# Softmax denominators of the last four slots: summed by TensorE per chunk instead of by GpSimd

## Chip, cores and metric

The kernel runs on one core of a Trainium2 chip. The metric is the device time of one execution in microseconds (us). Before the change it is 1859.81 us, the median of three runs (1859.74 to 1862.59). The chip's engines go by these names below: PE is TensorE (PEld its weight loads), DVE is VectorE, ACT is ScalarE, POOL is GpSimd, SP issues the DMAs.

## What is computed

One layer of a perceiver: a cross attention, a differential self attention and a mixture of eight experts, each added to the running `x`. Only the cross attention is touched. Cut to it, the reference is:

```python
q = (query @ wq.T + bq).reshape(B, SQ, H, HD).transpose(0, 2, 1, 3)
k = (key @ wk.T + bk).reshape(B, -1, H, HD).transpose(0, 2, 1, 3)
v = (value @ wv.T + bv).reshape(B, -1, H, HD).transpose(0, 2, 1, 3)
scores = jnp.einsum('bhqd,bhkd->bhqk', q, k) / jnp.sqrt(HD)
attn = jax.nn.softmax(scores, axis=-1)
ctx = jnp.einsum('bhqk,bhkd->bhqd', attn, v)
```

Here B = 8 batches, 128 queries, 2048 keys, 16 heads of 32 (HD), width 512, all in float32.

## The kernel before

`cross_attention` cuts the attention into 32 **slots**, one for each batch and group of four heads, and each slot into four **chunks** of 512 keys, so chunk number n = 4·slot + c runs from 0 to 127. All engines follow one hand-written calendar of **beats**: functions such as `score_step(beat)` or `value_step(beat)` say which chunk has its turn at a beat, and each engine walks over the beats in program order, waiting on semaphores where it needs another engine. A slot takes eight beats. For 32 · 8 beats TensorE also projects the keys and values (`keys`, `values`, `transposes`), one unit at each beat, and this fills it. From beat 256 on the projections are over, and slots 28 to 31 are still to be finished; that stretch is called the **tail** here.

What happens to a chunk, with the lines of the profile:

- PE, `column_scores` (L587): 16 matmuls write scores, keys on the partitions, to the PSUM tile `psS`. There is one such tile, so PE waits until ACT has moved the chunk before (`s_moved`).
- DVE (L759, L762): four maxima over `psS` into `mx`.
- ACT, "move" (L713): copies `psS` to one of six buffers of `s` (`BUFS = 6`), so it waits for the readers of chunk n − 6.
- Once in a slot, PE turns `mx` (`turn("M", ...)`, L619), DVE reduces it (L726), ACT spreads it (L700), PE turns it back (`turn("B", ...)`), ACT copies it to `mb` (L692).
- DVE (L733): subtracts `mb` from the chunk. ACT (L705): the exponential, in place.
- PE, `outputs` (L601): 16 matmuls add values times exponentials to `psO[:, 0:P]`.
- POOL (L512, L517): sums the exponentials of the slot's 16 key tiles into `acc`; 7 additions of 128x1024 in a slot, two for each chunk but the first, which has one.
- PE, `denominators` (L611): when POOL has finished the slot, 8 matmuls with a block of ones sum `acc` over the partitions into `psO[:, P:2*P]`.
- DVE (L740, L742, L747): reciprocal, product and bias of the slot; SP writes it to `o_scratch`.

The order of DVE at an even beat is: reduction, subtraction of chunk n, the slot's end, maxima of chunk n + 5. The order of PE is: `outputs`, `denominators`, `column_scores`, projection, turns. The units that pass through PSUM (transposes, projections, the two turns) use three banks `work` in turn, by a table RING made in advance:

```python
        BANKS = 3
        RING = {}
        for beat in range(FIRST, LAST):
            if (x0 := transposed(beat)) is not None:
                RING["T", *x0] = len(RING)
```

After the cross attention comes a barrier, and then `output_projection` (its transposes are L772, its products L43 to L45, POOL's additions L831).

Of the kernel before, what the change touches and what calls it, by code (L numbers as in the profile page):

```python
# [11 lines left out]
ACT = mybir.ActivationFunctionType  # L12
# [3 lines left out]
P = 128  # L16
B = 8
# [300 lines left out]
def cross_attention(nc, x, ctx_in, w, q_d, o_d, cin, shared):  # L318

    with ExitStack() as ctx:  # L320
# [12 lines left out]
        ADDS = 2 * CHUNK - 1  # L333
        MAXIMA = CHUNK * CHUNK

        def steps(beat, first, every, count):

            n, r = divmod(beat - first, every)
            return n if r == 0 and 0 <= n < count else None
# [32 lines left out]
        def sum_slot(beat):  # L372
            return steps(beat, 40, SLOT, SLOTS)
# [3 lines left out]


        BANKS = 3
        RING = {}  # L380
        for beat in range(FIRST, LAST):
            if (x0 := transposed(beat)) is not None:
                RING["T", *x0] = len(RING)
            if (x0 := projected(beat)) is not None:
                p0, u0 = x0
                RING["KV"[u0 // CHUNK], p0, u0 % CHUNK] = len(RING)
            if (s0 := turned_slot(beat)) is not None:
                RING["M", s0, 0] = len(RING)
            if (s0 := spread_slot(beat)) is not None:
                RING["B", s0, 0] = len(RING)  # L390
        UNITS = list(RING)

        def key_place(b, g, c):

# [106 lines left out]
        @block.gpsimd  # L501
        def _(pool):
            nc.gpsimd.memset(ones[:, :], 1.0).then_inc(const, 1)
            for n in range(SLOTS * CHUNK):
                m, c = divmod(n, CHUNK)
                buf = n % BUFS
                pool.wait_ge(exp_done, n + 1)
                if c == 0:

                    if m:  # L510
                        pool.wait_ge(od_full, m)
                    nc.gpsimd.tensor_tensor(acc[:, :, :], s[:, buf, 0:2, :], s[:, buf, 2:4, :],  # L512
                                            ALU.add).then_inc(sum_done, 1)
# [12 lines left out]
        def _(pe):  # L526
            pe.wait_ge(const, 1)

            def bank_of(unit):
                i = RING[unit]  # L530
                if i >= BANKS:
                    kind, m, n = UNITS[i - BANKS]
                    if kind == "T":
                        pe.wait_ge(split_done, m * CHUNK + n + 1)
                    elif kind == "K":
                        pe.wait_ge(k_done, m * CHUNK + n + 1)
                    elif kind == "V":
                        pe.wait_ge(v_done, m * CHUNK + n + 1)
                    elif kind == "M":
                        pe.wait_ge(top_done, m + 1)  # L540
                    else:
                        pe.wait_ge(mb_done, m + 1)
                return work[i % BANKS]

            def transposes(p, n):
                h, kk = divmod(n, 2)
# [44 lines left out]
            def outputs(n):  # L591
                m, c = divmod(n, CHUNK)
                b, g = divmod(m, G)
                pe.wait_ge(v_done, (b * CHUNK + c + 1) * CHUNK)
                if c == 0 and m:
                    pe.wait_ge(od_free, m)
                pe.wait_ge(exp_done, n + 1)
                for i in range(CHUNK):
                    at = value_places(b, c * CHUNK + i)[g]
                    for j in range(HG):  # L600
                        last = nc.tensor.matmul(psO[j * HD:(j + 1) * HD, 0:P],  # L601
                                                v[:, at + j * HD:at + (j + 1) * HD],
                                                s[:, n % BUFS, i, j * P:(j + 1) * P],
                                                start=c == 0 and i == 0, stop=c == CHUNK - 1 and i == CHUNK - 1)
                last.then_inc(pv_done, 1)

            def denominators(m):
                pe.wait_ge(sum_done, (m + 1) * ADDS)
# [13 lines left out]
            for beat in range(FIRST, LAST):  # L622
                if (x0 := transposed(beat)) is not None:
                    transposes(*x0)
                if (n := value_step(beat)) is not None:
                    outputs(n)
                if (m := sum_slot(beat)) is not None:
                    denominators(m)
                if (n := score_step(beat)) is not None:
                    column_scores(n)  # L630
                if (x0 := projected(beat)) is not None:
                    p, u = x0
                    if u < CHUNK:
# [17 lines left out]
        def _(act):  # L651
            act.wait_ge(bias_in, 32)
            for beat in range(FIRST, LAST):
                if (x0 := projected(beat - 1)) is not None:
                    p, u = x0
                    b, c = divmod(p, CHUNK)
                    if u < CHUNK:
                        i = RING["K", p, u]
                        act.wait_ge(work_full, i + 1)
                        if b:  # L660

                            act.wait_ge(s_full, ((b - 1) * G + c) * CHUNK + u + 1)
                        at = key_place(b, u, c)
                        nc.scalar.activation(kT[:, at:at + 512], work[i % BANKS][:, :], ACT.Identity,  # L664
                                             bias=bk[:, u:u + 1]).then_inc(k_done, 1)
                    else:
                        u -= CHUNK
                        i = RING["V", p, u]
                        act.wait_ge(work_full, i + 1)
                        if b:  # L670

# [1 line left out]
                        at = value_places(b, c * CHUNK + u)  # L673
                        step = at[1] - at[0]
                        if step == P:
                            nc.scalar.activation(v[:, at[0]:at[0] + D], work[i % BANKS][:, :],
                                                 ACT.Copy).then_inc(v_done, 1)
                        else:
                            rows = v.rearrange("p (g r) -> p g r", r=step)
# [5 lines left out]
                            nc.scalar.activation(out, work[i % BANKS][:, :].rearrange("p (g r) -> p g r", g=G),  # L685
                                                 ACT.Copy).then_inc(v_done, 1)
                if (m := spread_slot(beat - 1)) is not None:
                    i = RING["B", m, 0]
                    act.wait_ge(work_full, i + 1)

                    reached(act, sub_done, m * CHUNK)
                    nc.scalar.activation(mb[:, :], work[i % BANKS][:, :], ACT.Copy).then_inc(mb_done, 1)  # L692
                if (x0 := transposed(beat)) is not None:
                    p, n = x0
                    i = RING["T", p, n]
                    act.wait_ge(work_full, i + 1)
                    nc.scalar.activation(context_place(cT[0], p, n), two(work[i % BANKS]), ACT.Copy).then_inc(hi_done, 1)  # L697
# [8 lines left out]
                if (n := move_step(beat)) is not None:  # L706

                    act.wait_ge(mx_done, CHUNK * (n + 1))
                    if n >= BUFS:

                        act.wait_ge(pv_done, n - BUFS + 1)
                        act.wait_ge(sum_done, sums_of(n - BUFS))
                    nc.scalar.activation(s[:, n % BUFS, :, :].rearrange("p t (j q) -> p t j q", j=HG),  # L713
                                         psS[:, :, :].rearrange("p j (t q) -> p t j q", t=CHUNK),
                                         ACT.Copy).then_inc(s_moved, 1)
# [2 lines left out]
        def _(dve):  # L718
            dve.wait_ge(bias_in, 32)
            for beat in range(FIRST, LAST):  # L720
                if (m := spread_slot(beat)) is not None:
                    i = RING["M", m, 0]
                    dve.wait_ge(work_full, i + 1)

                    reached(dve, spread_done, m - 1)
                    nc.vector.tensor_reduce(top[:, m % 2, :], work[i % BANKS][:, :].rearrange("p (j k) -> p j k", j=HG),  # L726
                                            AX.X, ALU.max).then_inc(top_done, 1)
                if (n := exp_step(beat)) is not None:
                    m, c = divmod(n, CHUNK)
# [6 lines left out]
                        ALU.subtract).then_inc(sub_done, 1)  # L736
                if (m := normal_slot(beat)) is not None:
                    g = m % G
                    dve.wait_ge(od_full, m + 1)
                    nc.vector.reciprocal(rD[:, :], psO[:, P:2 * P]).then_inc(rd_done, 1)  # L740
                    dve.wait_ge(rd_done, m + 1)
                    nc.vector.tensor_tensor(oq[:, :], psO[:, 0:P], rD[:, :], ALU.mult).then_inc(od_free, 1)  # L742
                    dve.wait_ge(od_free, m + 1)
# [5 lines left out]
                if (x0 := transposed(beat)) is not None:  # L749
                    p, n = x0  # L750
                    dve.wait_ge(hi_done, p * CHUNK + n + 1)
                    nc.vector.tensor_tensor(context_place(cT[1], p, n), two(work[RING["T", p, n] % BANKS]),  # L752
                                            f32(context_place(cT[0], p, n)), ALU.subtract).then_inc(split_done, 1)
                if (n := score_step(beat)) is not None:
                    dve.wait_ge(s_full, n + 1)
# [945 lines left out]
```

## Time and profile before

| | |
|---|---|
| median of three runs | 1859.81 us |
| the profiled execution, its own time | 1860.6 us |
| its span in the trace | 1858.2 us |
| PE busy | 1716.2 us (92%) |
| DVE busy | 1224.5 us (66%) |
| ACT busy | 962.7 us (52%) |
| POOL busy | 776.3 us (42%) |
| mean granted TensorE clock | 0.955 of full |

The span is what the trace covers, and the profiled execution's own time is 2.4 us longer: what lies around the span. Busy shares are means over stages with different limits, so the stretch that the change touches has to be read by itself: where an engine is idle there, what ended that idle time, and when each slot ends.

### The profile page before, as it was taken

The numbers are of one execution on the slowest core, as the hardware profiler recorded it, in microseconds if no ns is written. First come the engines' busy times: TensorE is split into PE (matmuls) and PEld (weight loads), VectorE is DVE, ScalarE is ACT, GpSimd is POOL, SyncE is SP. The second block draws the span as 40 slices with busy tenths as digits, with TensorE's granted clock in tenths as the row PEclk, the third lists the DMA queues.
The fourth block names the chain that finished last, engine by engine and source line by source line (L and its number), as shares of the span: only waits on it lengthen the run. The fifth ranks groups of instructions, "written<-read, shape, count | busy, mean of one in ns | idle before, by whom it ended". The sixth has DMA issues, their size and how long they took to land. (4 is left out here: it accounts for less than half of the span.)

```text
span 1858.2 us, 36962 instructions
## 1 busy us (share of the span) xinstructions
PE 1716.2 (92%) x15305; PEld 1377.4 (74%) x15320; DVE 1224.5 (66%) x1631; ACT 962.7 (52%) x1470; POOL 776.3 (42%) x343
## 2 busy tenths in 40 slices
PE   6899999999999999999999997538999689879999
PEld 5688888888888888888888875437887466658886
DVE  5126887887887787787787788957332677753223
ACT  2236666666666666666666665533220677731000
POOL 0002555555555555555555555662000466622210
PEclk9999999999999999999999998658999899989999
DMA  4211111111111111110110102103650533201101
GB/s 162 69 46 38 38 29 40 38 28 40 38 30 38 38 34 34 38 40 28 38 41 27 38 7 71 44 29 131 201 179 14 159 92 90 68 24 46 45 23 45
DMA packets 104189, 104.94 MB, mean 56 GB/s; under 512 B 7263, under 2 KB 72799, under 8 KB 104044
## 3 DMA queue, kind: packets, MB, share of 16 engines
q1 hardware_dynamic: 104044, 102.83, 18.2%
q8 instruction: 113, 1.85, 0.4%
q14 instruction: 32, 0.26, 0.0%
HBM read 79.74 MB, written 23.07 MB: 55 GB/s over the span
## 5 line engine op out<-in xcount | busy, mean ns | idle before, releaser
L517 POOL TENSOR_TENSOR b_acc<-b_acc,b_s 128x1024 f32<-128x1024 f32 x192 | 525.7, 2738 | 294.6 <-ACT b_s L705 282.3
L733 DVE TENSOR_TENSOR b_s<-b_s,b_mb 128x2048 f32<-128x2048 f32 x128 | 372.5, 2912 | 15.7 <-ACT b_mb L692 15.7
L762 DVE TENSOR_TENSOR b_mx<-b_psS,b_mx 128x512 f32<-128x512 f32 x480 | 331.1, 690 | 44.2 <-PE b_psS L587 31.1
L705 ACT ACTIVATE b_s<-b_s 128x2048 f32<-128x2048 f32 x128 | 245.1, 1915 | 89.3 <-DVE b_s L733 89.3
L713 ACT ACTIVATE b_s<-b_psS 128x2048 f32<-128x2048 f32 x128 | 241.1, 1884 | 50.8 <-DVE b_mx L762 50.4
L43 PE MATMUL b_work<-cT,wkT 128*128 128x512 f32 x512 | 211.0, 412 | 0.0
L43 PE MATMUL b_work<-wvT,cT 128*128 128x512 f32 x512 | 209.4, 409 | 0.0
L512 POOL TENSOR_TENSOR b_acc<-b_s 128x1024 f32<-128x1024 f32 x32 | 80.8, 2525 | 290.8 <-PE b_psO L611 179.8
L44 PE MATMUL b_work<-cT,wkT 128*128 128x512 f32 x512 | 201.0, 393 | 0.0
L45 PE MATMUL b_work<-cT,wkT 128*128 128x512 f32 x512 | 200.7, 392 | 0.0
L45 PE MATMUL b_work<-wvT,cT 128*128 128x512 f32 x512 | 200.2, 391 | 0.0
L44 PE MATMUL b_work<-wvT,cT 128*128 128x512 f32 x512 | 200.0, 391 | 0.0
L587 PE MATMUL b_psS<-b_q,b_kT 32*128 32x128 f32 x4096 | 157.4, 292 | 15.1 <-ACT b_s L713 15.1
L664 ACT ACTIVATE b_kT<-b_work,b_bk 128x512 f32<-128x512 f32 x128 | 88.1, 688 | 157.4 <-PE b_work L45 155.0
L587 PEld LDWEIGHTS b_psS<-b_q,b_kT 32*128 32x128 f32 x4096 | 132.3, 194 | 41.6 <-issue 41.4
L601 PE MATMUL b_psO<-b_s,v_sb 128*32 128x128 f32 x4096 | 147.3, 289 | 15.6 <-ACT b_s L705 12.9
L601 PEld LDWEIGHTS b_psO<-b_s,v_sb 128*32 128x32 f32 x4096 | 111.9, 115 | 44.3 <-issue 43.7
L752 DVE TENSOR_TENSOR cT<-b_work,cT 128x512 fp32r<-128x512 f32 x128 | 87.3, 683 | 84.4 <-ACT cT L697 84.4
L1648 DVE SCALAR_TENSOR_TENSOR x<-f_ps,f_gate,x 128x512 f32<-128x512 f32 x64 | 47.9, 750 | 119.8 <-PE f_ps L45 119.3
L43 PEld LDWEIGHTS b_work<-cT,wkT 128*128 128x128 f32 x512 | 96.6, 189 | 30.1 <-issue 5.6
L43 PEld LDWEIGHTS b_work<-wvT,cT 128*128 128x128 f32 x512 | 96.1, 188 | 24.4
L45 PEld LDWEIGHTS b_work<-cT,wkT 128*128 128x128 f32 x512 | 96.7, 189 | 21.5
(221 smaller groups left out, 3036.7 us busy)
## 6 DMA issues: line engine op xcount, KB each, us to landing
cin<-in_ctx SPq DMA_DIRECT2D x64, 512.0 KB, 3.7
q_scratch<-d_st SPq DMA_DIRECT2D x32, 256.0 KB, 2.5
k_scratch<-d_st SPq DMA_DIRECT2D x32, 256.0 KB, 2.5
e_q<-q_scratch SPq DMA_DIRECT2D x16, 512.0 KB, 3.5
k_sb<-k_scratch SPq DMA_DIRECT2D x64, 128.0 KB, 3.6
experts_sb<-in_L_ffn_expert_w SPq DMA_DIRECT2D x8, 1024.0 KB, 5.2
x_sb<-in_x SPq DMA_DIRECT2D x2, 1024.0 KB, 7.1
q_scratch<-a_q SPq DMA_DIRECT2D x4, 512.0 KB, 3.2
```

What stands on the lines that cost most here:

```text
L43: nc.tensor.matmul(out, lhs[0], rhs[0], start=first, stop=False)
L44: nc.tensor.matmul(out, lhs[0], rhs[1], start=False, stop=False)
L45: return nc.tensor.matmul(out, lhs[1], rhs[0], start=False, stop=last)
L517: nc.gpsimd.tensor_tensor(acc[:, :, :], acc[:, :, :], s[:, buf, 2 * i:2 * i + 2, :], ALU.add).then_inc(sum_done, 1)
L587: last = nc.tensor.matmul(psS[:, j, t * P:(t + 1) * P], kT[h, at + t * P:at + (t + 1) * P], q[h, m % 3, :], start=True, stop=True)
L601: last = nc.tensor.matmul(psO[j * HD:(j + 1) * HD, 0:P], v[:, at + j * HD:at + (j + 1) * HD], s[:, n % BUFS, i, j * P:(j + 1) * P], start= ...
L664: nc.scalar.activation(kT[:, at:at + 512], work[i % BANKS][:, :], ACT.Identity, bias=bk[:, u:u + 1]).then_inc(k_done, 1)
L705: nc.scalar.activation(part, part, ACT.Exp, scale=SCALE).then_inc(exp_done, 1)
L713: nc.scalar.activation(s[:, n % BUFS, :, :].rearrange("p t (j q) -> p t j q", j=HG), psS[:, :, :].rearrange("p j (t q) -> p t j q", t=CHUN ...
L733: nc.vector.tensor_tensor(s[:, n % BUFS, :, :], s[:, n % BUFS, :, :], mb[:, :].rearrange("p (o n) -> p o n", o=1).broadcast_to([P, CHUNK, ...
L752: nc.vector.tensor_tensor(context_place(cT[1], p, n), two(work[RING["T", p, n] % BANKS]), f32(context_place(cT[0], p, n)), ALU.subtract).t ...
L762: nc.vector.tensor_tensor(mx[:, :, :], part, mx[:, :, :], ALU.max).then_inc(mx_done, 1)
```

## The change

In the last four slots (`TAIL = SLOTS - 4`, so slots 28 to 31, those of the tail) POOL does nothing. Right behind the 16 matmuls of `outputs`, for each chunk, PE does 16 more matmuls with the block of ones as weights and the exponentials of the chunk as the moving side, and so adds the denominators of the slot up in PSUM. They need a bank of their own, for which the third `work` bank is used: from beat 256 on the two turns use two banks. The semaphore `pv_done` now counts up after these matmuls. The end of the slot on DVE waits for it in place of `od_full`, and ACT's move no longer waits for POOL's sums of chunks of these slots.

```diff
+        TAIL = SLOTS - 4
...
+        def enter(unit, beat):
+            banks = BANKS if beat < SLOTS * SLOT else BANKS - 1
+            RING[unit] = len(RING)
+            BANK[unit] = RING[unit] % banks
+            LAST_IN[unit] = after[BANK[unit]]
+            after[BANK[unit]] = unit
...
-            for n in range(SLOTS * CHUNK):
+            for n in range(TAIL * CHUNK):
                 m, c = divmod(n, CHUNK)
                 buf = n % BUFS
                 pool.wait_ge(exp_done, n + 1)
...
+                if m >= TAIL:
+                    last = chunk_denominators(n)
                 last.then_inc(pv_done, 1)
+
+            def chunk_denominators(n):
+                c = n % CHUNK
+                if n == TAIL * CHUNK:
+                    wait_evicted(after[BANKS - 1])
+                for i in range(CHUNK):
+                    for j in range(HG):
+                        last = nc.tensor.matmul(work[BANKS - 1][j * HD:(j + 1) * HD, 0:P], ones[:, :],
+                                                s[:, n % BUFS, i, j * P:(j + 1) * P],
+                                                start=c == 0 and i == 0, stop=c == CHUNK - 1 and i == CHUNK - 1)
+                return last
...
-                if (m := sum_slot(beat)) is not None:
+                if (m := sum_slot(beat)) is not None and m < TAIL:
                     denominators(m)
...
                         act.wait_ge(pv_done, n - BUFS + 1)
-                        act.wait_ge(sum_done, sums_of(n - BUFS))
+                        if (n - BUFS) // CHUNK < TAIL:
+                            act.wait_ge(sum_done, sums_of(n - BUFS))
...
-                    dve.wait_ge(od_full, m + 1)
-                    nc.vector.reciprocal(rD[:, :], psO[:, P:2 * P]).then_inc(rd_done, 1)
+                    if m < TAIL:
+                        dve.wait_ge(od_full, m + 1)
+                    else:
+                        dve.wait_ge(pv_done, (m + 1) * CHUNK)
+                    sums = psO[:, P:2 * P] if m < TAIL else work[BANKS - 1][:, 0:P]
+                    nc.vector.reciprocal(rD[:, :], sums).then_inc(rd_done, 1)
```

The order of TensorE in the middle of the tail, from the end of slot 28 to the turn of slot 30's maxima, before the change (`b_psO<-b_s,v_sb` are the outputs, `b_psS` the scores, `b_ones` with `b_acc` the denominators; an `x15` row is the rest of the group above it):

```order
L611 MATMUL b_psO<-b_acc,b_ones 32x128 [waits b_sum_done]
L611 MATMUL b_psO<-b_acc,b_ones 32x128 x7
L587 MATMUL b_psS<-b_q,b_kT 128x128 [waits b_s_moved,b_k_done]
L587 MATMUL b_psS<-b_q,b_kT 128x128 x15
L601 MATMUL b_psO<-b_s,v_sb 32x128 [waits b_exp_done,b_od_free,b_v_done]
L601 MATMUL b_psO<-b_s,v_sb 32x128 x15
L601 MATMUL b_psO<-b_s,v_sb 32x128 [waits b_exp_done,b_v_done]
L601 MATMUL b_psO<-b_s,v_sb 32x128 x15
L587 MATMUL b_psS<-b_q,b_kT 128x128 [waits b_s_moved,b_k_done]
L587 MATMUL b_psS<-b_q,b_kT 128x128 x15
L619 MATMUL b_work<-ident,b_mx 128x128 [waits b_mx_done,b_v_done]
L619 MATMUL b_work<-ident,b_mx 128x128 x3
```

And after it:

```order
L600 MATMUL b_psS<-b_q,b_kT 128x128 [waits b_s_moved,b_k_done]
L600 MATMUL b_psS<-b_q,b_kT 128x128 x15
L614 MATMUL b_psO<-b_s,v_sb 32x128 [waits b_exp_done,b_od_free,b_v_done]
L614 MATMUL b_psO<-b_s,v_sb 32x128 x15
L628 MATMUL b_work<-b_s,b_ones 32x128 x16
L614 MATMUL b_psO<-b_s,v_sb 32x128 [waits b_exp_done,b_v_done]
L614 MATMUL b_psO<-b_s,v_sb 32x128 x15
L628 MATMUL b_work<-b_s,b_ones 32x128 x16
L600 MATMUL b_psS<-b_q,b_kT 128x128 [waits b_s_moved,b_k_done]
L600 MATMUL b_psS<-b_q,b_kT 128x128 x15
L645 MATMUL b_work<-ident,b_mx 128x128 [waits b_mx_done,b_top_done]
L645 MATMUL b_work<-ident,b_mx 128x128 x3
```

The eight matmuls on `acc` with their wait for POOL are gone, and 16 matmuls without a wait of their own stand behind each group of outputs, ahead of the next scores. The turn waits for the reduction of the slot before instead of for a value unit.

The end of the cross attention on TensorE, before and then after (the last two chunks of slot 31):

```order
L601 MATMUL b_psO<-b_s,v_sb 32x128 [waits b_exp_done,b_v_done]
L601 MATMUL b_psO<-b_s,v_sb 32x128 x15
L601 MATMUL b_psO<-b_s,v_sb 32x128 [waits b_exp_done,b_v_done]
L601 MATMUL b_psO<-b_s,v_sb 32x128 x15
L611 MATMUL b_psO<-b_acc,b_ones 32x128 [waits b_sum_done]
L611 MATMUL b_psO<-b_acc,b_ones 32x128 x7
```

```order
L614 MATMUL b_psO<-b_s,v_sb 32x128 [waits b_exp_done,b_v_done]
L614 MATMUL b_psO<-b_s,v_sb 32x128 x15
L628 MATMUL b_work<-b_s,b_ones 32x128 x16
L614 MATMUL b_psO<-b_s,v_sb 32x128 [waits b_exp_done,b_v_done]
L614 MATMUL b_psO<-b_s,v_sb 32x128 x15
L628 MATMUL b_work<-b_s,b_ones 32x128 x16
```

The last thing that PE does for a slot no longer waits for POOL. The orders of DVE, ACT and SP are the same instructions in the same order as before; only the waits named above differ.

## Rows read from the trace of the kernel before

**Rows 1.** The page, its 40 slices: TensorE and its granted clock.

```profile
PE   6899999999999999999999997538999689879999
...
PEclk9999999999999999999999998658999899989999
```

**Rows 2.** Stretches: us, busy (x instructions) of PE, PEld, DVE, ACT, POOL, PE clock, DMA share, GB/s.

```profile
1000.00:1100.00 100.00, 100.00 (x1118) 80.72 (x1117) 79.86 (x81) 65.68 (x63) 53.81 (x20) 1.00 0.09 26
...
1135.90:1166.50 30.60, 15.98 (x266) 12.80 (x262) 28.40 (x26) 16.26 (x10) 20.49 (x8) 0.64 0.30 106
1166.50:1196.83 30.33, 17.03 (x287) 13.76 (x281) 28.14 (x25) 16.26 (x10) 20.30 (x7) 0.61 0.01 4
1196.83:1226.00 29.17, 12.21 (x201) 9.46 (x196) 25.10 (x18) 12.51 (x8) 19.14 (x7) 0.56 0.25 66
1226.00:1247.40 21.40, 7.58 (x132) 5.80 (x123) 8.09 (x5) 3.82 (x2) 18.00 (x6) 0.50 0.05 13
```

**Rows 3.** Timeline of DVE in slot 29: start, us, what [idle before <-releaser].

```profile
1166.42 2.85 DVE L762 TENSOR_TENSOR b_mx<-b_psS,b_mx 128x512 f32<-128x512 f32 x4
1169.19 4.31 DVE L733 TENSOR_TENSOR b_s<-b_s,b_mb 128x2048 f32<-128x2048 f32 x1
...
1177.55 0.69 DVE L726 TENSOR_REDUCE b_top<-b_work 128x4 f32<-128x512 f32 x1 [1.27 <-PE b_work L619]
1178.16 4.32 DVE L733 TENSOR_TENSOR b_s<-b_s,b_mb 128x2048 f32<-128x2048 f32 x1
...
1185.17 3.85 DVE L733 TENSOR_TENSOR b_s<-b_s,b_mb 128x2048 f32<-128x2048 f32 x1
...
1192.24 2.28 DVE L733 TENSOR_TENSOR b_s<-b_s,b_mb 128x2048 f32<-128x2048 f32 x1
...
1195.75 1.08 DVE L747 TENSOR_SCALAR b_o<-b_oq,b_bv 128x128 f32<-128x128 f32 x1
```

**Rows 4.** Timeline of POOL in the same slot.

```profile
1166.56 4.80 POOL L517 TENSOR_TENSOR b_acc<-b_acc,b_s 128x1024 f32<-128x1024 f32 x2
...
1184.50 6.75 POOL L517 TENSOR_TENSOR b_acc<-b_acc,b_s 128x1024 f32<-128x1024 f32 x2 [4.17 <-ACT b_s L705]
1192.56 4.19 POOL L512 TENSOR_TENSOR b_acc<-b_s 128x1024 f32<-128x1024 f32 x1 [1.31 <-PE b_psO L611]
```

**Rows 5.** Timeline of PE, just before the tail (first two rows) and in slot 29.

```profile
1125.12 1.08 PE L601 MATMUL b_psO<-b_s,v_sb 128*32 128x128 f32 x32
1126.13 1.17 PE L587 MATMUL b_psS<-b_q,b_kT 32*128 32x128 f32 x32
...
1176.43 1.09 PE L619 MATMUL b_work<-ident,b_mx 128*128 128x128 f32 x4 [3.34 <-DVE b_mx L762]
1177.44 1.93 PE L601 MATMUL b_psO<-b_s,v_sb 128*32 128x128 f32 x32
1179.31 2.09 PE L587 MATMUL b_psS<-b_q,b_kT 32*128 32x128 f32 x32
1181.33 0.96 PE L619 MATMUL b_work<-ident,b_spread 128*128 128x128 f32 x4
1184.57 1.19 PE L601 MATMUL b_psO<-b_s,v_sb 128*32 128x128 f32 x32 [2.28 <-ACT b_s L705]
1187.31 2.09 PE L587 MATMUL b_psS<-b_q,b_kT 32*128 32x128 f32 x32 [1.55 <-ACT b_s L713]
1191.30 1.08 PE L611 MATMUL b_psO<-b_acc,b_ones 128*32 128x128 f32 x16 [1.91 <-POOL b_acc L517]
```

**Rows 6.** Timeline of ACT: the last value copy, and a move in slot 29.

```profile
1133.04 0.60 ACT L685 ACTIVATE v_sb<-b_work 128x512 f32<-128x512 f32 x1 [0.34 <-PE b_work L45]
...
1192.36 1.88 ACT L713 ACTIVATE b_s<-b_psS 128x2048 f32<-128x2048 f32 x1 [1.39 <-DVE b_mx L762]
```

**Rows 7.** Timeline of all engines at the end of the cross attention.

```profile
1226.05 18.52 POOL L517 TENSOR_TENSOR b_acc<-b_acc,b_s 128x1024 f32<-128x1024 f32 x6
1227.58 1.28 SPq L497 DMA_DIRECT2D o_sb<-o_scratch  x3
...
1234.64 1.94 PE L601 MATMUL b_psO<-b_s,v_sb 128*32 128x128 f32 x32 [2.42 <-ACT b_s L705]
...
1244.62 1.08 PE L611 MATMUL b_psO<-b_acc,b_ones 128*32 128x128 f32 x16 [8.04 <-POOL b_acc L517]
1245.78 0.96 DVE L740 RECIPROCAL b_rD<-b_psO 128x128 f32<-128x128 f32 x1 [13.22 <-PE b_psO L611]
...
1247.10 0.29 DVE L747 TENSOR_SCALAR b_o<-b_oq,b_bv 128x128 f32<-128x128 f32 x1
...
1255.09 0.76 PE L43 MATMUL c_ps<-c_woT,c_oT 128*128 128x512 f32 x1 [3.26 <-issue]
...
1264.12 10.04 POOL L831 TENSOR_TENSOR x<-x,c_bo 128x512 f32<-128x512 f32 x8 [9.27 <-issue]
```

More of the change, by code:

```diff
@@ L379, in cross_attention @@
         BANKS = 3
-        RING = {}
+        RING, BANK, LAST_IN = {}, {}, {}
+        def enter(unit, beat):
[4 more added lines that the diff above has]
+            after[BANK[unit]] = unit
+        after = [None] * BANKS
         for beat in range(FIRST, LAST):
             if (x0 := transposed(beat)) is not None:
-                RING["T", *x0] = len(RING)
+                enter(("T", *x0), beat)
             if (x0 := projected(beat)) is not None:
                 p0, u0 = x0
-                RING["KV"[u0 // CHUNK], p0, u0 % CHUNK] = len(RING)
+                enter(("KV"[u0 // CHUNK], p0, u0 % CHUNK), beat)
             if (s0 := turned_slot(beat)) is not None:
-                RING["M", s0, 0] = len(RING)
+                enter(("M", s0, 0), beat)
             if (s0 := spread_slot(beat)) is not None:
-                RING["B", s0, 0] = len(RING)
-        UNITS = list(RING)
+                enter(("B", s0, 0), beat)
         def key_place(b, g, c):
@@ L527, in _, with wait_evicted @@
             pe.wait_ge(const, 1)
[L529 to L532, printed above, removed]
+            def wait_evicted(unit):
+                if unit is not None:
+                    kind, m, n = unit
                     if kind == "T":
@@ L542, in bank_of @@
                         pe.wait_ge(mb_done, m + 1)
-                return work[i % BANKS]
+            def bank_of(unit):
+                wait_evicted(LAST_IN[unit])
+                return work[BANK[unit]]
             def transposes(p, n):
@@ L657, in _ @@
                     if u < CHUNK:
-                        i = RING["K", p, u]
+                        i, bank = RING["K", p, u], work[BANK["K", p, u]]
                         act.wait_ge(work_full, i + 1)
@@ L663, in _ @@
                         at = key_place(b, u, c)
-                        nc.scalar.activation(kT[:, at:at + 512], work[i % BANKS][:, :], ACT.Identity,
+                        nc.scalar.activation(kT[:, at:at + 512], bank[:, :], ACT.Identity,
                                              bias=bk[:, u:u + 1]).then_inc(k_done, 1)
@@ L667, in _ @@
                         u -= CHUNK
-                        i = RING["V", p, u]
+                        i, bank = RING["V", p, u], work[BANK["V", p, u]]
                         act.wait_ge(work_full, i + 1)
@@ L675, in _ @@
                         if step == P:
-                            nc.scalar.activation(v[:, at[0]:at[0] + D], work[i % BANKS][:, :],
+                            nc.scalar.activation(v[:, at[0]:at[0] + D], bank[:, :],
                                                  ACT.Copy).then_inc(v_done, 1)
@@ L684, in _ @@
                                 out = rows[:, :, at[0]:at[0] + P]
-                            nc.scalar.activation(out, work[i % BANKS][:, :].rearrange("p (g r) -> p g r", g=G),
+                            nc.scalar.activation(out, bank[:, :].rearrange("p (g r) -> p g r", g=G),
                                                  ACT.Copy).then_inc(v_done, 1)
                 if (m := spread_slot(beat - 1)) is not None:
-                    i = RING["B", m, 0]
+                    i, bank = RING["B", m, 0], work[BANK["B", m, 0]]
                     act.wait_ge(work_full, i + 1)
                     reached(act, sub_done, m * CHUNK)
-                    nc.scalar.activation(mb[:, :], work[i % BANKS][:, :], ACT.Copy).then_inc(mb_done, 1)
+                    nc.scalar.activation(mb[:, :], bank[:, :], ACT.Copy).then_inc(mb_done, 1)
                 if (x0 := transposed(beat)) is not None:
                     p, n = x0
-                    i = RING["T", p, n]
+                    i, bank = RING["T", p, n], work[BANK["T", p, n]]
                     act.wait_ge(work_full, i + 1)
-                    nc.scalar.activation(context_place(cT[0], p, n), two(work[i % BANKS]), ACT.Copy).then_inc(hi_done, 1)
+                    nc.scalar.activation(context_place(cT[0], p, n), two(bank), ACT.Copy).then_inc(hi_done, 1)
                 if (m := spread_slot(beat)) is not None:
@@ L721, in _ @@
                 if (m := spread_slot(beat)) is not None:
-                    i = RING["M", m, 0]
+                    i, bank = RING["M", m, 0], work[BANK["M", m, 0]]
                     dve.wait_ge(work_full, i + 1)
                     reached(dve, spread_done, m - 1)
-                    nc.vector.tensor_reduce(top[:, m % 2, :], work[i % BANKS][:, :].rearrange("p (j k) -> p j k", j=HG),
+                    nc.vector.tensor_reduce(top[:, m % 2, :], bank[:, :].rearrange("p (j k) -> p j k", j=HG),
                                             AX.X, ALU.max).then_inc(top_done, 1)
@@ L751, in _ @@
                     dve.wait_ge(hi_done, p * CHUNK + n + 1)
-                    nc.vector.tensor_tensor(context_place(cT[1], p, n), two(work[RING["T", p, n] % BANKS]),
+                    nc.vector.tensor_tensor(context_place(cT[1], p, n), two(work[BANK["T", p, n]]),
                                             f32(context_place(cT[0], p, n)), ALU.subtract).then_inc(split_done, 1)
```

## The prediction

> **What bounds the kernel now.** I read the slices first: TensorE is busy at 0.9 or more nearly everywhere and its clock full, but both sink in the slices around 1160 to 1250 us [rows 1]. That is the tail. The stretches tell what kind of a dip it is: in the steady part TensorE is busy 100 of 100 us at full clock; in the tail it is busy 16 to 17 of some 30 us a slot at a granted clock of 0.61 to 0.64, while DVE is busy 28 [rows 2]. I cut the stretches where DVE finishes slots 27 to 31 (1135.9, 1166.5, 1196.8, 1226.0, 1247.4), so the four lengths, 30.6, 30.3, 29.2 and 21.4 us, are what the slots cost; from the true end of slot 27 (1136.2) it is 111.2 us in all. In the first two DVE is the bound, with 28.1 to 28.4 of 30.5; in the last one POOL is, with 18.0 of 21.4.
>
> Then the timelines. DVE's subtraction takes 2.28 us when POOL rests (1192.24, as POOL starts again at 1192.56) and 4.31, 4.32 and 3.85 us when POOL adds beside it [rows 3, 4]; POOL suffers in turn, its pair of additions going from 4.80 to 6.75. The same holds of the small bias operation: 1.08 us in the tail, 0.29 us when POOL is silent [rows 3, 7]. TensorE's rows tell its clock: 16 output matmuls (x32 in the trace) take 1.08 us at 2.4 GHz and 1.93 at 1.2 GHz, the scores 1.17 and 2.09 [rows 5]. At the end, PE's last outputs are done at 1236.6, POOL at 1244.6; PE waits 8.04 us for it, DVE 13.22 [rows 7].
>
> **What the change moves.**
>
> 1. POOL's 28 additions of the tail go. First effect: DVE. In a slot the subtractions shrink from 4.31 + 4.32 + 3.85 + 2.28 = 14.76 to 4 · 2.28 = 9.12, the bias operation by 0.79; together 6.4 us off DVE's path, 30.3 - 6.4 = 23.9 if nothing takes their place [rows 2, 3]. Second effect: the 8.04 us wait at the end goes.
>
> 2. PE gets 16 matmuls for each of the 16 chunks. No row shows this form on `s`; the nearest are the outputs (same count, shape, columns): 1.93 us at 1.2 GHz, 1.02 net at full clock (1.08 less what overlaps the next row). The other bound is twice the group on `acc` (x16 in 1.08): 2.16 [rows 5]. I take 1.93 / 1.02, the row with the same count. The eight matmuls on `acc` (1.08) go.
>
> 3. What takes the place of DVE is a loop: scores, four maxima (2.85), move (1.88), next scores, since there is one score tile. At full clock it is 1.17 + 2.85 + 1.88 + three hand-overs of 0.06 = 6.1, or 24.3 for a slot; with the one meeting of turn and reduction that today leaves DVE idle [rows 3], I get **25.2** a slot. At half clock the loop is 7.0, or 28.0, and the new matmuls enter it: behind the slot's end PE does outputs and denominators of two chunks (4 · 1.93 = 7.7) and only then scores (2.09), 9.8 where the loop had 7.0: +2.8. At the turn PE does turn, outputs, denominators, scores, 1.09 + 3.86 + 2.09 = 7.0, where only the move (1.88) and the scores stood between the maxima: +3.1. So **33.9** for slot 29; **30.6** for slot 28, whose first stretch still runs at full clock.
>
> 4. Slot 30 has scores for half of its time: 20.9 at full clock, 25.9 at half (today 29.2). Slot 31 begins with slot 30's product; PE then has 4 outputs and 4 denominators to do, and DVE 1.6 us: 8 · 1.02 + 1.6 = 9.8, with a wait for the exponential 10.1; at half clock 8 · 1.93 + 1.6 = 17.0 (16.9 in the walk). Today 21.4.
>
> 5. Sums: full clock 25.2 + 25.2 + 20.9 + 10.1 = 81.4; half clock 30.6 + 33.9 + 25.9 + 16.9 = 107.3; today 111.2. Slot 27's bias operation also loses its neighbour (-0.9).
>
> 6. Which clock? Today the clock falls at the tail's start and returns for moments: PE worked without a gap from 1176.43 to 1182.3, its outputs at 1184.57 took 1.19, nearly the full-clock value, and by 1187.31 the scores took 2.09 again [rows 5]. So it rose some 5 us into an unbroken stretch and fell after gaps of 2.28 and 1.55 us. After the change a slot holds two unbroken stretches of about 10 us (items 3 and the turn); I let the first 5 us of each run at half clock and the rest at full. That is 10 of 25.9 us of PE's half-clock work in a slot, a weight of 0.39: slot 28 is 25.2 + 0.39 · 5.4 = 27.3, slot 29 25.2 + 0.39 · 8.7 = 28.6, slot 30 20.9 + 0.39 · 5.0 = 22.9; slot 31, one stretch of 16 us, 10.1 + 0.31 · 6.8 = 12.2. Sum **91.0**. The gain is 111.2 - 91.0 + 0.9 = 21.1 us.
>
> The Trainium skill (TensorE: Matmul & The Clock Gate, "Why this matters for your kernels") says that the clock goes back when TensorE idles between bursts and asks for dense bursts. In the new tail the bursts lie close, so by it the full-clock sum holds all through (rival A). The rows here speak against it in part: the clock fell with gaps no longer than 2.28 us.
>
> 7. At nothing: the wait for the last value copy before the first denominators (done at 1133.64, before PE comes there [rows 6]); the turns' two banks, whose last tenant was read a slot earlier; the six buffers, whose move now waits for denominators of chunk n - 6, 1 us later than outputs alone and, at full clock, before the maxima are done; at half clock it is in item 3. SP's order is unchanged; its three reads behind slot 30's write end at 1228.9, 2.9 us after that slot [rows 7], and slot 31 still takes 12.
>
> 8. The rest of the kernel starts 21 us earlier, otherwise as it is: the output projection loads POOL's code and waits for its additions (at 1264.12) behind the barrier, in both kernels. Only the clock at its start may differ: its first products took 0.63 to 0.76 us, at half clock, for some 5 us from 1255.09 [rows 7], so -2.6 at best, +1 at worst; I take 0.
>
> The profiled execution took 1860.6: 1860.6 - 21.1 = 1839.5; the median lies 0.8 below it, so **1838.7**. A measurement of this kernel tells about 0.2%, 3.7 us, from no change.
>
> **The rivals.** In each price the same 0.8 is taken off.
>
> A. TensorE's clock stays full, chance 0.12: 111.2 - 81.4 + 0.9 = 30.7, **1829.1**. For it: PE is much busier. Against: at full clock its work is only about 14 of 25 us, as today's 16 of 30.
>
> B. The clock stays at half, 0.08: 107.3, gain 4.8, **1855.0**. For it: granted 0.50 in slot 31 today [rows 2]. Against: stretches of today's kind raised it.
>
> C. The subtractions stay at 4.3 us without POOL, that is, their length has another cause, 0.06: DVE then remains the bound at 30 a slot and only the end shrinks, by 8.04 less the last denominators and queued ones (4): **about 1856**. Against: 2.28 at 1192.24.
>
> D. Slower: TensorE becomes the bound, because the clock stays at half and the new groups cost more than outputs, 0.04. By item 3 nearly each stands in the path: of 16, 14.5 count. From case B (4.8 to spare) it breaks even at 1.93 + 4.8 / 14.5 = 2.26 us a group, near the bound of 2.16, is slower by 3.7 from 2.5, and at 2.9 costs 9.2: **1869**. It needs both at once.
>
> E. It does not do what it says: another stage, the barrier or a load, holds the time, 0.02: **1859.8**. Against: nothing ahead of the barrier but slot 31 ends late.
>
> **How the numbers follow.** The forecast (0.68) itself runs from 1832 (clock returns early, the projection starts warm) to 1847 (2.16 a group: +3; clock back only after 8 us: +3; start +1). With A the range is **1828 to 1848**, 0.8 of the chance; B to E lie outside. Faster by over 3.7: forecast, A, most of B and half of C: 0.89. Within: 0.07. Slower: 0.04.
>
> **What would show it.** Subtractions of 2.3 us all through the tail; no POOL rows between 1129 and the barrier; slots 28 and 29 of 27 to 29 us, with idle DVE before the maxima, released by the scores; denominators at 1.0 to 1.9 us; a mean clock of 0.7 to 0.85; slot 31 of 11 to 13 us, ended by PE. Wrong if subtractions stay above 3 us, if the slots reach 30 us, or if the output projection's own length changes by more than 3 us.

## The result

The changed kernel takes 1834.55 us (median of four runs, 1830.62 to 1840.81) against 1860.92 beside it: a ratio of 0.9861, with a 95% interval of 0.9827 to 0.9894. That is 26.4 us less; 1838.7 was forecast, with a range of 1828 to 1848. Two later measurements of the same kernel, told below, gave 1835.27 and 1834.17.

The slices of the page, after the change; the dip in the middle, which was 9975389996 for TensorE and 9998658999 for its clock [rows 1], is shallower:

```profile
PE   6899999999999999999999998567999689979999
...
PEclk9999999999999999999999999789999899999999
```

Stretches of the changed kernel, cut where VectorE (DVE) finishes slots 27 to 31, with the columns of [rows 2]; the profiled execution has a span of 1829.8 us and a time of 1831.57:

```profile
1134.27:1161.16 26.89, 15.04 (x389) 13.23 (x383) 21.90 (x25) 16.02 (x11) 0.00 (x0) 0.85 0.36 122
1161.16:1188.56 27.40, 16.43 (x399) 14.29 (x396) 22.00 (x24) 16.27 (x11) 0.00 (x0) 0.81 0.02 4
1188.56:1210.78 22.22, 13.96 (x313) 11.60 (x313) 16.57 (x17) 12.51 (x9) 0.00 (x0) 0.80 0.33 87
1210.78:1221.08 10.30, 8.64 (x256) 8.37 (x247) 5.93 (x5) 4.25 (x3) 0.00 (x0) 0.83 0.11 29
```

The tail is 86.8 us where it was 111.2. GpSimd (POOL) is silent, VectorE is busy 22 us in each of slots 28 and 29 instead of 28, and TensorE's clock is 0.80 to 0.85 instead of 0.50 to 0.64. VectorE's timeline in slot 29, which answers to [rows 3]:

```profile
1161.65 2.87 DVE L793 TENSOR_TENSOR b_mx<-b_psS,b_mx 128x512 f32<-128x512 f32 x4 [0.49 <-PE b_psS L600]
1164.43 2.28 DVE L760 TENSOR_TENSOR b_s<-b_s,b_mb 128x2048 f32<-128x2048 f32 x1
1167.81 2.87 DVE L793 TENSOR_TENSOR b_mx<-b_psS,b_mx 128x512 f32<-128x512 f32 x4 [1.10 <-PE b_psS L600]
...
1188.27 0.29 DVE L778 TENSOR_SCALAR b_o<-b_oq,b_bv 128x128 f32<-128x128 f32 x1
```

Every subtraction takes 2.28 us, the bias operation 0.29, and VectorE now waits for TensorE's scores before nearly each group of maxima. TensorE in the same slot, which answers to [rows 5], and then in slot 31:

```profile
1159.50 2.09 PE L600 MATMUL b_psS<-b_q,b_kT 32*128 32x128 f32 x32 [4.98 <-ACT b_s L740]
1161.52 1.94 PE L614 MATMUL b_psO<-b_s,v_sb 128*32 128x128 f32 x32
1163.23 1.14 PE L628 MATMUL b_work<-b_s,b_ones 128*32 128x128 f32 x32
1164.19 1.05 PE L614 MATMUL b_psO<-b_s,v_sb 128*32 128x128 f32 x32
...
1210.56 1.39 PE L614 MATMUL b_psO<-b_s,v_sb 128*32 128x128 f32 x32 [4.28 <-DVE b_oq L773]
1211.65 2.01 PE L628 MATMUL b_work<-b_s,b_ones 128*32 128x128 f32 x32
1213.35 1.70 PE L614 MATMUL b_psO<-b_s,v_sb 128*32 128x128 f32 x32
...
1218.33 1.08 PE L628 MATMUL b_work<-b_s,b_ones 128*32 128x128 f32 x32
```

The scores after a gap of 4.98 us run at 1.2 GHz (2.09), and some 3.7 us later the clock is back: the denominators at 1163.23 take 1.14. The slot ends on TensorE at 1219.4 and not on GpSimd, 8 us behind the outputs, as in [rows 7].

Where the span's 28.4 us went: 24.4 in the four slots; 0.9 in slot 27's bias operation, which took 1.25 with GpSimd beside it and takes 0.29 now; 1.0 ahead of the tail and 2.1 behind it (the rest took 608.7 us instead of 610.8), where the instructions are the same in both. These last two are no larger than what the same parts differ by among the profiles below: where GpSimd is silent in the whole tail, slot 27 ended between 1133.4 and 1136.4 us (seven profiles) and the rest took 606 to 609.3; in run 3 it took 614.8.

### The profile page after: what moved, and what is told of

It reads as the page before. It is cut to its first block and busy times, and to the rows that moved or that the text cites. A ratio compares the mean times of both kernels' runs of the same rounds, so it can differ in the third digit from the quotient of the medians.

```text
span 1829.8 us, 37829 instructions
## 1 busy us (share of the span) xinstructions
PE 1710.6 (93%) x15768; PEld 1376.8 (75%) x15768; DVE 1200.3 (66%) x1631; ACT 962.1 (53%) x1470; POOL 695.6 (38%) x315
## 5 line engine op out<-in xcount | busy, mean ns | idle before, releaser
L528 POOL TENSOR_TENSOR b_acc<-b_acc,b_s 128x1024 f32<-128x1024 f32 x168 | 458.6, 2730 | 268.5 <-ACT b_s L731 258.1
L760 DVE TENSOR_TENSOR b_s<-b_s,b_mb 128x2048 f32<-128x2048 f32 x128 | 350.9, 2743 | 15.7 <-ACT b_mb L718 15.7
L523 POOL TENSOR_TENSOR b_acc<-b_s 128x1024 f32<-128x1024 f32 x28 | 66.9, 2389 | 281.2 <-PE b_psO L637 171.0
L600 PE MATMUL b_psS<-b_q,b_kT 32*128 32x128 f32 x4096 | 152.0, 285 | 16.1 <-ACT b_s L740 16.1
L600 PEld LDWEIGHTS b_psS<-b_q,b_kT 32*128 32x128 f32 x4096 | 127.6, 188 | 41.4 <-issue 41.2
L614 PE MATMUL b_psO<-b_s,v_sb 128*32 128x128 f32 x4096 | 143.5, 282 | 6.1 <-DVE b_oq L773 4.3
L43 PEld LDWEIGHTS b_work<-cT,wkT 128*128 128x128 f32 x512 | 96.6, 189 | 30.1 <-issue 5.6
L45 PEld LDWEIGHTS b_work<-cT,wkT 128*128 128x128 f32 x512 | 96.6, 189 | 21.4
```

Of the source, the lines that this page charges most:

```text
L43: nc.tensor.matmul(out, lhs[0], rhs[0], start=first, stop=False)
L45: return nc.tensor.matmul(out, lhs[1], rhs[0], start=False, stop=last)
L600: last = nc.tensor.matmul(psS[:, j, t * P:(t + 1) * P], kT[h, at + t * P:at + (t + 1) * P], q[h, m % 3, :], start=True, stop=True)
L614: last = nc.tensor.matmul(psO[j * HD:(j + 1) * HD, 0:P], v[:, at + j * HD:at + (j + 1) * HD], s[:, n % BUFS, i, j * P:(j + 1) * P], start= ...
L760: nc.vector.tensor_tensor(s[:, n % BUFS, :, :], s[:, n % BUFS, :, :], mb[:, :].rearrange("p (o n) -> p o n", o=1).broadcast_to([P, CHUNK, ...
```

## The experiments

In short; the tail is slots 28 to 31 of each run's profiled execution. Before took 1858.74 us beside runs 1 to 4, 1860.06 beside 5 to 7, 1859.18 beside 8 and 9.

| run | median us | ratio [95% interval] | slots 28, 29, 30, 31 | tail |
|---|---|---|---|---|
| 1 the change again | 1835.27 | 0.9868 [0.9845, 0.9891] | 27.7, 29.0, 22.7, 11.2 | 90.6 |
| 2 GpSimd beside | 1854.86 | 0.9982 [0.9971, 0.9993] | 30.9, 29.2, 27.5, 13.8 | 101.5 |
| 3 last slot alone | 1846.65 | 0.9932 [0.9910, 0.9954] | 30.3, 30.3, 28.4, 10.7 | 99.7 |
| 4 without the groups | 1830.94 | 0.9847 [0.9824, 0.9871] | 26.4, 27.1, 22.2, 10.1 | 85.7 |
| 5 groups twice | 1844.72 | 0.9924 [0.9908, 0.9939] | 28.2, 30.0, 24.3, 14.8 | 97.2 |
| 6 gaps filled | 1828.38 | 0.9832 [0.9818, 0.9845] | 25.6, 25.5, 21.2, 10.1 | 82.4 |
| 7 the change, third time | 1834.17 | 0.9863 [0.9848, 0.9878] | 28.0, 29.1, 22.2, 10.3 | 89.6 |
| 8 last slot, gaps filled | 1841.16 | 0.9898 [0.9880, 0.9916] | 27.7, 30.1, 26.3, 10.1 | 94.2 |
| 9 filled again | 1827.93 | 0.9842 [0.9818, 0.9866] | 25.5, 25.5, 21.2, 10.1 | 82.3 |

**1 and 7: the change itself again.** No edit.

> The changed kernel itself, as the ruler for the others. In its first profile slots 28 to 31 took 26.9, 27.4, 22.2 and 10.3 us, 86.8 together, against 111.2 before. Theory: the tail is set by TensorE's clock in some stretches, which comes and goes at moments that are not tied to the program, so another execution should have the four slots within 84 to 90 us, and the median should be 1831 to 1840 us. Rival (the first profile was a lucky one): a tail of over 92 us and a median near or above the 1838.7 of the prediction.

> The changed kernel again, beside the two others on the same chip. As before, 1831 to 1840 us, with a tail of 84 to 91 us.

The medians lie within what was expected. The tail came out at 90.6 and 89.6 us, the first just over the 90 of the first expectation. So the first profile, at 86.8, was on the short side, and the 91.0 of the prediction on the long side. The difference between the three is mostly slots 28 and 29, where the clock came back earlier or later in a stretch of work. TensorE at the first turn of the tail, in run 7:

```profile
1142.49 1.08 PE L645 MATMUL b_work<-ident,b_mx 128*128 128x128 f32 x4 [3.07 <-DVE b_mx L793]
1143.51 1.94 PE L614 MATMUL b_psO<-b_s,v_sb 128*32 128x128 f32 x32
1145.21 1.93 PE L628 MATMUL b_work<-b_s,b_ones 128*32 128x128 f32 x32
1147.08 1.51 PE L600 MATMUL b_psS<-b_q,b_kT 32*128 32x128 f32 x32
```

And the same place in the first profile of the change:

```profile
1143.35 1.09 PE L645 MATMUL b_work<-ident,b_mx 128*128 128x128 f32 x4 [3.07 <-DVE b_mx L793]
1144.37 1.94 PE L614 MATMUL b_psO<-b_s,v_sb 128*32 128x128 f32 x32
1146.07 1.18 PE L628 MATMUL b_work<-b_s,b_ones 128*32 128x128 f32 x32
1147.18 1.17 PE L600 MATMUL b_psS<-b_q,b_kT 32*128 32x128 f32 x32
```

There the denominators took 1.18 us, not 1.93, and the scores 1.17, not 1.51: the same program, with the clock back some 2 us sooner after the turn began.

**2: is it GpSimd that makes the subtractions long?** GpSimd adds as often and as much as before in the last four slots, on keys that no longer change, and nobody waits for it.

```diff
+            for n in range(TAIL * CHUNK, SLOTS * CHUNK):
+                m, c = divmod(n, CHUNK)
+                pool.wait_ge(exp_done, n + 1)
...
+                for i in range(1 if c == 0 else 2):
...
+                    nc.gpsimd.tensor_tensor(acc[:, :, :], acc[:, :, :],
+                                            kT[:, i * 1024:(i + 1) * 1024].rearrange("p (a b) -> p a b", a=2),
+                                            ALU.add).then_inc(sum_done, 1)
```

> The changed kernel, with GpSimd doing additions of the same number and shape as before in the last four slots, on other data, and nobody waits for them. Theory (the subtractions of VectorE were long because GpSimd added beside them): three of four subtractions in slots 28 to 30 go back from 2.28 to 3.8 to 4.4 us, VectorE is the bound again, slots 28 to 30 take about 30, 30 and 26 us, slot 31 about 13, the tail 100 instead of 87, and the time is 11 to 15 us above the changed kernel. Rival (their length had another cause, or the wait at the end was nearly all of the gain): subtractions of 2.3 us, and within 3 us of the changed kernel.

VectorE and GpSimd in this run:

```profile
1138.41 4.32 DVE L770 TENSOR_TENSOR b_s<-b_s,b_mb 128x2048 f32<-128x2048 f32 x1
1147.39 4.32 DVE L770 TENSOR_TENSOR b_s<-b_s,b_mb 128x2048 f32<-128x2048 f32 x1
1154.59 3.67 DVE L770 TENSOR_TENSOR b_s<-b_s,b_mb 128x2048 f32<-128x2048 f32 x1
...
1160.96 4.15 DVE L770 TENSOR_TENSOR b_s<-b_s,b_mb 128x2048 f32<-128x2048 f32 x1
...
1169.32 2.33 DVE L770 TENSOR_TENSOR b_s<-b_s,b_mb 128x2048 f32<-128x2048 f32 x1
1177.98 2.98 DVE L770 TENSOR_TENSOR b_s<-b_s,b_mb 128x2048 f32<-128x2048 f32 x1
...
1212.21 29.82 POOL L537 TENSOR_TENSOR b_acc<-b_acc,b_kT 128x1024 f32<-128x1024 f32 x9 [4.17 <-ACT b_s L741]
```

The long subtractions are back, although no wait between the two engines exists: all four in slot 28, and two of four (3.85 to 4.18 us) in slots 29 and 30, where the others took 2.33 to 3.05; three of four had been expected. The rival, another cause of the length, falls. With them nearly the whole gain is gone: the median is 19.6 us above run 1, more than the 11 to 15 expected.

Of these 19.6 us the profile accounts for 15.2, measured against the mean of the three profiles of the change: 12.5 in the tail (101.5 - 89.0), 1.0 ahead of it, where slot 27's bias operation takes 1.23 us again, and 1.7 behind it (610.2 instead of 608.5). The additions, held up in turn, run to 1242.0, 4.8 us past the last slot's end at 1237.2; no more than the 1.7 us of that are left at the end of the kernel. The profiled execution took 1849.17, the lowest of this run's ten and 5.7 us below their median; what the others lost more stays open.

**3: the end alone.** `TAIL = SLOTS - 1` in place of `SLOTS - 4`.

> Only slot 31 gets the new way (TAIL = SLOTS - 1); slots 28 to 30 are as before. Theory (two separate gains): slots 28 to 30 stay at 30.3, 30.3 and about 28.5 us, and slot 31 falls from 21.4 to 10 to 13 us, so 8 to 11 us of the 26 are gained: 1850 to 1853 us. Rival (GpSimd's lateness at the end is the whole matter): nearly the full gain, below 1840 us.

```profile
1137.06:1167.34 30.28, 15.85 (x255) 12.77 (x248) 28.09 (x25) 16.26 (x10) 20.25 (x7) 0.63 0.31 107
1167.34:1197.65 30.31, 17.31 (x287) 14.01 (x281) 28.11 (x26) 16.26 (x10) 20.28 (x7) 0.61 0.01 4
1197.65:1226.00 28.35, 11.63 (x188) 8.91 (x182) 24.27 (x18) 12.08 (x8) 16.05 (x6) 0.56 0.26 68
1226.00:1236.74 10.74, 9.06 (x256) 8.79 (x248) 5.93 (x5) 4.25 (x3) 0.00 (x0) 0.81 0.10 27
```

These stretches of run 3 are [rows 2] again in slots 28 and 29, and slot 31 is 10.7 us for 21.4. The median gains 12.1, a little over the 8 to 11; in the profile the gain of slots 30 and 31 is 11.5 (the profiled execution was the slowest of the four, 1853.34, by the long rest named above). So the two halves of the change are about equal: 12.1 us at the end, and 11.4 more (to run 1) by relieving VectorE in slots 28 to 30.

**4: what do the new matmuls cost?** `chunk_denominators` is not called.

> The changed kernel without the new matmuls: the denominators of the last four slots are left out. Theory (the new matmuls mostly lie beside other work and also bring TensorE's clock back): the tail shortens by only 3 to 6 us of its 87, with a lower granted clock than in the changed kernel, and scores at 2.09 us more often. Rival (the 16 new groups stand in the path of TensorE, 0.9 to 1.9 us each): the tail shortens by 14 us or more.

The median is 4.3 us below run 1 and 3.2 below run 7; the tail is 85.7, against 89.0. So 16 groups of 0.87 us or more cost the path some 3 to 4 us. This is a rough size: the executions of run 4 (1828.67 to 1832.78) still overlap those of run 7 (1831.89 to 1835.46), and its one profile has a tail 1.1 to 4.9 us shorter than the three of the change. The clock in the four stretches of run 4 was 0.74, 0.69, 0.65 and 0.50, lower than the 0.73 to 0.85 with the groups: what they take as work they partly give back as clock.

**5: twice as many.** Each group is done twice.

```diff
-                    last = chunk_denominators(n)
+                    chunk_denominators(n, 0)
+                    last = chunk_denominators(n, 1)
```

> The changed kernel with each new group of matmuls done twice, so the denominators of the last four slots come out doubled. Theory (the groups lie half beside the scores loop, half in it, and more work also keeps the clock up): 16 more groups of 0.9 to 1.9 us lengthen the tail by 4 to 12 us, mostly in slot 31, where nothing is beside them (4 groups, 3.5 to 7 us). Rival (TensorE is the bound of the tail): 16 groups of 0.9 us or more in full, 14 to 30 us.

It costs 10.6 us over run 7. In the profiles 7.6 of that lie in the tail, inside the 4 to 12, and 2.6 ahead of it, where the two programs do the same. Of the 7.6, 4.5 fall on slot 31 (14.8 for 10.3), where 4 groups stand in the open; the other twelve cost 3.1 together, far less than their own length. So the sum of TensorE's work does not bound slots 28 to 30.

**6 and 9: what is the clock worth?** Behind scores and outputs (in slots 28 to 30) that are followed by a gap, TensorE does further matmuls, into a `work` bank that is free there: 16 for each 0.9 us of gap.

```diff
+            def filler(groups):
+                bank = work[BANK["M", TAIL + 1, 0]]
+                for r in range(groups * CHUNK * HG):
+                    j = r % HG
+                    nc.tensor.matmul(bank[j * HD:(j + 1) * HD, 0:P], ones[:, :], ident[:, :], start=True, stop=True)
...
                     outputs(n)
+                    if n >= TAIL * CHUNK and n % CHUNK == 3:
+                        filler(1 if n < 123 else 3 if n == 123 else 0)
...
                     column_scores(n)
+                    if n == 119:
+                        wait_evicted(LAST_IN["M", TAIL + 1, 0])
+                    if n >= 119:
+                        filler((0, 4, 0, 2)[n % CHUNK])
```

> The changed kernel with further matmuls, whose results nobody reads, in the gaps of TensorE in the tail: 16 on constant data for each 0.9 us of a gap, so that the engine hardly rests. Theory (what is left of the tail above its best is scores and outputs at 1.2 GHz in the path): the granted clock is 1.00 in the tail, scores take 1.17 us throughout, slots 28 to 31 take about 25, 25, 21 and 10 us, 81 instead of 87 to 91, and the time is 5 to 10 us below the changed kernel. Rival (the fillers delay what stands behind them as much as they bring): no difference, or slower by up to 5 us.

> The filled kernel again beside it: 1826 to 1829 us, slots 28 to 31 at 25.5, 25.5, 21.2 and 10.1 us in each execution, since the clock no longer depends on the moment.

Stretches of run 6, and then rows of TensorE in it:

```profile
1135.99:1161.56 25.57, 19.83 (x625) 17.73 (x620) 21.89 (x25) 15.92 (x11) 0.00 (x0) 1.00 0.36 128
1161.56:1187.08 25.52, 20.17 (x625) 17.85 (x620) 21.91 (x26) 16.19 (x11) 0.00 (x0) 1.00 0.02 6
1187.08:1208.24 21.16, 16.34 (x465) 14.81 (x460) 16.46 (x17) 12.39 (x9) 0.00 (x0) 0.92 0.34 93
1208.24:1218.35 10.11, 7.39 (x256) 6.64 (x247) 5.94 (x5) 4.26 (x3) 0.00 (x0) 1.00 0.11 29
```

```profile
1154.85 3.70 PE L652 MATMUL b_work<-ident,b_ones 128*32 128x128 f32 x128
1159.90 1.17 PE L600 MATMUL b_psS<-b_q,b_kT 32*128 32x128 f32 x32 [1.35 <-ACT b_s L752]
```

Instead of 4.98 us of idling and scores of 2.09, TensorE spends 3.7 us on work that nobody reads, idles 1.35, and does the scores in 1.17. The tail is 82.4 us, and the median 5.8 below run 7: the fastest version. In run 9 the median was 1827.93, with the same four lengths to 0.1 us in its profile (1824.68); its executions spread from 1824.68 to 1833.59, more than the 1826 to 1829 expected. Only one of them was profiled, so where the others lost their time is not shown. That parts outside the tail vary by microseconds is: see the ends of slot 27 and the rests under the result.

**8: is the clock worth anything while GpSimd adds?** Run 3 with the fillers.

> As in the run of the last slot alone, so GpSimd still adds in slots 28 to 30, and with the filling matmuls in TensorE's gaps there. Theory (TensorE's clock is worth something only once VectorE has been relieved of GpSimd): with the clock at 1.00 slots 28 and 29 still take 30.3 us each, since VectorE is busy 28 of them, and the time stays within 3 us of the 1846.65 of the run without fillers. Rival (the clock by itself makes the tail shorter, whatever GpSimd does): slots 28 and 29 of 27 to 28 us and a time of about 1840 us.

The median is 5.5 us below run 3: neither the theory (within 3 us) nor the rival (about 1840 with both slots shorter). Slot 29 kept its length (30.1), but slots 28 and 30 became 2.6 and 2.1 us shorter. The clock of 1.00 that the theory assumed was not reached either: the four stretches had 0.94, 0.83, 0.85 and 0.88. VectorE and GpSimd in slot 28, first in run 8, then in run 3:

```profile
1147.53 0.69 DVE L765 TENSOR_REDUCE b_top<-b_work 128x4 f32<-128x512 f32 x1 [0.81 <-PE b_work L645]
1148.14 2.28 DVE L772 TENSOR_TENSOR b_s<-b_s,b_mb 128x2048 f32<-128x2048 f32 x1
...
1145.87 13.69 POOL L528 TENSOR_TENSOR b_acc<-b_acc,b_s 128x1024 f32<-128x1024 f32 x4 [4.17 <-ACT b_s L743]
```

```profile
1148.17 0.69 DVE L753 TENSOR_REDUCE b_top<-b_work 128x4 f32<-128x512 f32 x1 [1.27 <-PE b_work L645]
1148.78 4.21 DVE L760 TENSOR_TENSOR b_s<-b_s,b_mb 128x2048 f32<-128x2048 f32 x1
...
1146.06 4.79 POOL L528 TENSOR_TENSOR b_acc<-b_acc,b_s 128x1024 f32<-128x1024 f32 x2 [4.17 <-ACT b_s L731]
```

With the turn at full clock the reduction starts 0.46 us sooner after it, and the subtraction starts 2.27 us after GpSimd's pair instead of 2.72: just before the first addition ends (some 2.4 us) instead of just behind it. In run 8 the subtraction takes 2.28 and GpSimd is held up: its four additions of this stretch follow each other without a break and take 13.69 us, where run 3 has 4.79 and 6.74 for the two pairs. In run 3 it is the other way round. The other slots fit. In slot 30 the subtraction starts 2.27 us after the pair in run 8 and takes 2.28, and 2.63 after it in run 3 and takes 4.30; in slot 29 of run 8 it starts 2.99 us after it, takes 3.97, and the slot stays long. Whichever is there first when the first addition ends goes first. So a faster clock changed who waits for whom. My reading that the clock is worth nothing while VectorE is the bound was wrong.

## Why the prediction was right

The forecast case happened: faster, by 26.4 us where 21.1 was worked out against the profiled execution, and inside the range. Against the three profiles of the change together, the tail gave 22.2 us (111.2 - 89.0) where 20.2 was worked out; the rest of the 26.4 lies ahead of the tail and behind it.

- **Item 1, the relief of VectorE,** held to the hundredth: 2.28 us for each subtraction, 0.29 for the bias operation. Run 2 shows the cause, which in the prediction was read off three rows only. One of them it read wrongly: the subtraction at 1192.24 does not take 2.28 us because GpSimd rests. GpSimd's addition from 1192.56 lies over it and takes 4.19 us [rows 4], where the same addition takes 2.39 and 2.36 with no subtraction beside it (at 1100.83 and 1133.76 in the same trace). The subtraction was there first, and GpSimd waited.
- **Item 2, the new groups,** had the right kind and nearly the right size: at full clock they follow each other by 0.87 us (1134.05, 1134.92, 1135.80, 1136.67 in the changed kernel), where 1.02 was taken; at half clock the row takes 1.93 as taken, with 1.70 to 1.87 from start to start.
- **Items 3 and 4, the loop of scores, maxima and move,** is what now sets the slots. The full-clock lengths 25.2, 25.2, 20.9 and 10.1 could be tried by the fillers and measured 25.6, 25.5, 21.2 and 10.1 (clock 1.00, but 0.92 in slot 30). The half-clock lengths were not tried. The idle time of VectorE before the maxima, released by the scores, is the sign that was named.
- **Item 4, slot 31,** has the 10.1 partly by luck. Its sum is eight groups of 1.02 us and 1.6 us of VectorE; in run 6 the groups take 0.87 each, and waits for the last exponentials make up the difference. Run 4 has no denominator groups and a clock of 0.50, and its slot 31 is 10.1 us as well; its TensorE also waits for the last two exponentials (0.87 and 0.26 us). So at full clock the subtractions and exponentials set the end of this slot, and not TensorE's work. The stretch of slot 31 in run 4, then the last outputs of run 6:

```profile
1210.61:1220.69 10.08, 7.29 (x128) 5.98 (x120) 5.93 (x5) 4.25 (x3) 0.00 (x0) 0.50 0.10 28
```

```profile
1214.73 1.08 PE L614 MATMUL b_psO<-b_s,v_sb 128*32 128x128 f32 x32 [0.24 <-ACT b_s L743]
```

- **Item 6, the clock,** is the term that was mis-sized. It let the first 5 us of each unbroken stretch run at half clock: 27.3, 28.6, 22.9 and 12.2, 91.0 in all. Three profiles gave 86.8, 90.6 and 89.6, mean 89.0. Slots 28 and 29 were right (27.5 and 28.5 in the mean); slot 31 was taken as 12.2 and was 10.3 to 11.2, because half clock held for only some 3 us there in the two shorter cases, and the groups at full clock are shorter than taken (in run 1 half clock held for 5 us, and the slot was 11.2). That slot 29 came out right is a mean: in the first profile half clock held for 3.7 and 2.7 us of its two stretches; in run 7 it held for some 5 and 3 us, and scores at 1181.87, behind a gap of 2.22 us, took 2.04 once more.
- **Item 8, nothing behind the tail,** was 2 us off: the rest took 610.8 us in the profile before and 608.7, 608.4 and 608.2 in the three of the change. The 2 us do not come from the output projection: from slot 31 to the self attention's first write to `q_scratch` it is 58.0 us in the first profile of the change and 57.0 before, since GpSimd stood idle for 10.20 us ahead of its additions instead of 9.27 and began them 1.5 us later (that this is the loading of code no row shows). They come from the self attention, 157.7 us for 159.6 between its first and last load of `e_q`, and from the experts, 197.3 for 198.5. Both do the same in the two kernels. There is one profile of before only, and such parts vary by as much elsewhere, so whether the change has a hand in it stays open.
- **Rival A (full clock)** did not happen by itself; the fillers made it happen and gave 82.4 us, the 81.4 of its sum to 1 us, with work added to TensorE. The reasoning for it from the Trainium skill (TensorE: Matmul & The Clock Gate, "Why this matters for your kernels"), that longer idling between bursts sends the clock back, fits the runs: after the gap of 4.98 us the scores take 2.09, with the gap filled down to 1.35 they take 1.17.
- **Rival B (half clock)** is out with granted clocks of 0.73 to 0.85 in the three profiles, **C** by run 2, **E** by run 3, where slot 31 alone is 10.7 us shorter and the median 12.1 us lower. **D** needed the groups in the path at half clock; doubling them cost 0.5 us a group in the tail (0.66 in the median), and removing them gave back 0.2 to 0.3.

## What to carry to other kernels

Read the duration of one engine's operation with and without its neighbour at work before calling that neighbour free: here GpSimd, "only" 42% busy over the kernel and in the trace waited for by nobody but the denominators, cost VectorE 6.4 us of each 30 us slot. Work that moves to an engine with gaps can cost a quarter of its length, as here some 3 to 4 us for 16 groups of about 0.9 us or more, since it fills waits and keeps TensorE's clock up; 16 groups more already cost 7.6 in the tail. And where short bursts of TensorE stand in a loop with long waits between them, filling the waits with matmuls that nobody reads may pay by itself: 5.8 us here.

## What was not expected of the hardware

VectorE's subtraction (both inputs in SBUF) and GpSimd's addition hold each other up as wholes, and a difference of half a microsecond in the start decides which of them waits: 2.28 against 4.21 us for the same subtraction in runs 8 and 3. The lengths add up that way in [rows 3, 4] too: GpSimd's pair from 1184.50 takes 6.75 us, which is its own 4.80 and nearly the whole 2.28 of the subtraction that came between (7.08), and that subtraction takes 3.85, its own 2.28 and most of the 1.73 that were left of the first addition (4.01). The maxima, which read one input from PSUM, took 2.85 to 2.87 us with and without GpSimd. The Trainium skill (SBUF — State Buffer, "Who interferes with whom") says just this: the two share a port pair as an exclusive lock, and order of issue decides who blocks. The rows agree, also with what it says of instructions with one SBUF input: the maxima have one PSUM and one SBUF input and were not slowed. The bias operation has one SBUF tensor as input and went from 0.29 to 1.08 us all the same; the page says that such operations can run in a mode that takes the shared pair too, which no row here can show.

Executions of the changed kernel spread over 10 us (1830.62 to 1840.81), with mean granted clocks of 0.977 and 0.969 at 1831.57 and 1840.81. Before, where VectorE bound the slots, thirteen executions beside run 1 also spread over 8.3 us (1853.92 to 1862.18), so the spread did not come with the change.
